# Weight preparation of a graph attention kernel: from GpSimd to VectorE by quarters, and the second adjacency product between the first masked ones

## What is computed

```python
# N = M = 4096, D = 128; adj holds 0 and 1, about 0.2% of them 1
e   = layernorm(x) @ a1 + (input2 @ a2).T          # N x M
e   = where(e > 0, e, 0.2 * e)
att = softmax(where(adj > 0, e, -9e15), axis=1)
att = 0.1 * att * sum(adj, axis=1, keepdims=True) + 0.9 * adj
x   = x + att @ input2
x   = x + layernorm(x) @ weight.T + bias
```

## Time and profile before

| | |
|---|---|
| time, median of 3 runs | 422.19 us (421.56 to 422.73) |
| the profiled execution's own time | 422.5 us |
| its span, first to last instruction | 420.7 us |
| mean granted TensorE clock | 0.972 |
| PE busy | 372.3 us (88%) |
| DVE busy | 359.4 us (85%) |
| ACT busy | 300.8 us (72%) |
| POOL busy | 127.2 us (30%) |

### The profile page before, as it was taken

The page is one execution under the profiler, slowest core; times in us unless marked ns, Lnnn a source line. Parts: engine busy times, 40 slices in busy tenths (PEclk is TensorE's granted clock), DMA queues, the critical chain, the costliest instruction groups (busy, mean ns, idle before and its releaser), DMA issues.

```text
span 420.7 us, 9474 instructions
## 1 busy us (share of the span) xinstructions
PE 372.3 (88%) x3237; PEld 322.4 (77%) x3237; DVE 359.4 (85%) x925; ACT 300.8 (72%) x534; POOL 127.2 (30%) x201
## 2 busy tenths in 40 slices
PE   0072759998999999999999999999999999999992
PEld 0061648876888888888888888888888888888881
DVE  3999999999999799897979797979898897979653
ACT  2465946999887969595959596987969595957000
POOL 2589931141414040505041221404040505010101
PEclk9996889998999999999999999999999999999996
DMA  6963173385583737473746556473737373600000
GB/s 229 423 241 104 78 291 137 123 302 182 176 301 119 287 142 247 154 274 109 275 154 240 196 209 227 151 285 107 281 148 240 143 276 107 221 15 0 15 2 27
DMA packets 17338, 76.11 MB, mean 181 GB/s; under 512 B 1936, under 2 KB 8608, under 8 KB 9120
## 3 DMA queue, kind: packets, MB, share of 16 engines
q1 hardware_dynamic: 17312, 75.78, 50.3%
HBM read 73.66 MB, written 2.11 MB: 180 GB/s over the span
## 4 chain that ended last, share of the span: by engine, by line
PE 75%; DVE 13%; ACT 4%; issue 3%; DMA 2%; POOL 1%; SPq 0%; POOLq 0%; ACTq 0%; DVEq 0%
PE acc_u L645 24%; PE acc_v L645 24%; PE acc_y L645 23%; DVE plus L789 3%; ACT steep L485 3%; DVE plus L925 2%; DVE weights_u L972 2%; PE small L639 2%; DMA plus<-in 2%; DVE plus L797 1%; PE small L625 1%; ACT adj_b L475 1%; PE turned L614 1%; DVE minus L800 1%; DVE minus L964 1%
## 5 line engine op out<-in xcount | busy, mean ns | idle before, releaser
L485 ACT ACTIVATE steep<-s_bc,steep_s 128x256 bf16<-128x256 f32 x376 | 156.0, 495 | 2.4 <-DVE plus L797 2.4
L645 PE MATMUL acc_y<-weights_y,adj_b 128*128 128x258 f16 x1024 | 123.7, 279 | 10.0 <-ACT adj_b L475 10.0
L645 PE MATMUL acc_u<-weights_u,plus 128*128 128x258 f16 x1024 | 122.5, 276 | 6.7 <-DVE plus L797 6.7
L475 ACT ACTIVATE adj_b<-stage 128x2048 bf16<-128x2048 f32 x64 | 121.3, 1900 | 1.5 <-DMA stage<-adj 1.4
L645 PEld LDWEIGHTS acc_y<-weights_y,adj_b 128*128 128x128 bf16 x1024 | 101.8, 100 | 26.9 <-ACT adj_b L475 10.6
L645 PE MATMUL acc_v<-weights_v,minus 128*128 128x258 f16 x1024 | 120.5, 273 | 0.0
L645 PEld LDWEIGHTS acc_u<-weights_u,plus 128*128 128x128 bf16 x1024 | 100.7, 99 | 22.9 <-DVE plus L797 7.3
L645 PEld LDWEIGHTS acc_v<-weights_v,minus 128*128 128x128 bf16 x1024 | 100.0, 98 | 14.6
L800 DVE TENSOR_TENSOR minus<-adj_b,plus 128x2048 bf16<-128x2048 bf16 x64 | 78.4, 1225 | 2.2
L498 ACT ACTIVATE num<-acc_u,ac 128x129 f32<-128x129 f32 x32 | 11.5, 361 | 81.8 <-PE acc_u L645 81.8
L385 POOL TENSOR_SCALAR post_var<-post_mv 128x2 f32<-128x2 f32 x16 | 3.4, 213 | 207.7 <-DVE post_mv L866 207.7
(11 more groups left out here) (82 smaller groups left out, 299.6 us busy)
## 6 DMA issues: line engine op xcount, KB each, us to landing
stage<-adj SPq DMA_DIRECT2D x64, 1024.0 KB, 4.8
plus<-in SPq DMA_DIRECT2D x4, 512.0 KB, 7.2
x_pre<-x SPq DMA_DIRECT2D x16, 128.0 KB, 2.5
x_res<-x SPq DMA_DIRECT2D x16, 128.0 KB, 2.4
out<-late SPq DMA_DIRECT2D x16, 128.0 KB, 5.0
s_rows<-s_bc SPq DMA_DIRECT2D x16, 1.0 KB
a_bc<-a SPq DMA_DIRECT2D x2, 64.0 KB, 3.8
wt_sb<-w_t SPq DMA_DIRECT2D x1, 64.0 KB, 13.3
```

The source lines that it names most:

```text
L475: nc.scalar.activation(adj_b[b][:, q * QJ:(q + 1) * QJ, :], stage[:, q, :], ACT.Copy)\
L485: ins = nc.scalar.activation(steep[:, h, k, :], s1_bc[b][:, :], ACT.Relu, bias=steep_s2[:, jt:jt + 1], scale=STEEP)
L645: ins = nc.tensor.matmul(acc[:, 0:2 * WC], left[:, jt, cols(t)], right[:, jt, :, :].rearrange("p a b -> p (a b)"), start=(jt == 0), stop=( ...
```

## The change

POOL keeps only small instructions: a new function factor_columns writes the column D of w_u and w_v. low_y, value_v and low_v of all quarters are DVE's. In DVE's program the preparation of a quarter stands between the comparison and the combination of chunk 0's masks. RJ0 goes, so chunk 0's quarters are split as all the others. The val buffers become four, two for u and two for v, of D columns. PE does spread(0, 0) first, and y of chunk 1 by quarters between chunk 0's masked products. The load of x_pre[1] moves behind the first adjacency quarter. The epilogues of chunk 0 move behind two mask quarters of chunk 1 on DVE and on ACT.

```diff
 @@ SP
-            for b in range(2):
-                sp.dma_start(x_pre[b][:, :, :], x[b]).then_inc(xpre_landed[b], 16)
+            sp.dma_start(x_pre[0][:, :, :], x[0]).then_inc(xpre_landed[0], 16)
             for q in range(1, QUARTERS):
                 sp.dma_start(in2_f[:, q * QJ:(q + 1) * QJ, :], in2[:, q]).then_inc(in2_landed[q], 16)
             load_adj(0, 0)
+            sp.dma_start(x_pre[1][:, :, :], x[1]).then_inc(xpre_landed[1], 16)
 @@ POOL
+            def factor_columns():
+                pool.wait_ge(bd_ready, 1)
+                nc.gpsimd.tensor_scalar(d_lifted[:, :], bd[:, 1, :], WSCALE, 1.0, ALU.mult, ALU.mult)\
+                    .then_inc(lifted, 1)
+                nc.gpsimd.tensor_scalar(b_lifted[:, :], bd[:, 0, :], WSCALE, 1.0, ALU.mult, ALU.mult)\
+                    .then_inc(lifted, 1)
+                pool.wait_ge(lifted, 2)
+                nc.gpsimd.tensor_copy(w_u[:, :, 0, D], b_lifted[:, :]).then_inc(lifted, 1)
+                nc.gpsimd.tensor_copy(w_v[:, :, 0, D], d_lifted[:, :]).then_inc(lifted, 1)
+                pool.wait_ge(lifted, 4)
+                nc.gpsimd.tensor_tensor(b_rest[:, :], b_lifted[:, :], w_u[:, :, 0, D],
+                                        ALU.subtract).then_inc(lifted, 1)
+                nc.gpsimd.tensor_tensor(w_v[:, :, 1, D], d_lifted[:, :], w_v[:, :, 0, D],
+                                        ALU.subtract).then_inc(factor_cols, 1)
+                pool.wait_ge(lifted, 5)
+                nc.gpsimd.tensor_scalar(w_u[:, :, 1, D], b_rest[:, :], LOSCALE, 1.0, ALU.mult, ALU.mult)\
+                    .then_inc(factor_cols, 1)
 
             row_sums(0, 0)
-            low_y(0)
-            low_y(1)
+            factor_columns()
             factors(0, 0, True)
-            pool.wait_ge(bd_ready, 1)
...
-            value_v(0)
-            value_v(1)
-            low_v(0)
             row_sums(1, 1)
             factors(1, 1, False)
-            for q in range(1, QUARTERS - 1):
-                value_v(q + 1)
-                low_v(q)
-            low_v(QUARTERS - 1)
 @@ ACT (after the four casts of w_y's high part), the order in the new kernel
+            copy_spread(0, 0)
             cast(0, 0, 0)
             act.wait_ge(bd_arg_ready, 2)
             nc.scalar.activation(bd[:, :, :], bd_arg[:, :, :], ACT.Exp).then_inc(bd_ready, 1)
             cast(0, 1, 0)
             act.wait_ge(s2_signs, 2)
+            act.wait_ge(s1_ready, 1)
             high_u(0)
+            high_v(0)
+            sign_tests(0, 0, 0)
+            cast(0, 2, 0)
             high_u(1)
+            high_v(1)
+            sign_tests(0, 1, 0)
+            cast(0, 3, 0)
+            copy_spread(1, 1)
             high_u(2)
+            high_v(2)
+            sign_tests(0, 2, 0)
+            cast(1, 0, 1)
+            cast(1, 1, 1)
             high_u(3)
+            high_v(3)
+            sign_tests(0, 3, 0)
             cast(1, 2, 1)
             cast(1, 3, 1)
+            exps(0, 0)
...
-                order = ["first", "second", 0, 1, 2, 3] if isinstance(c, int) and c == 0 else \
+                order = [0, 1, "first", "second", 2, 3] if isinstance(c, int) and c == 0 else \
 @@ PE
+            spread(0, 0)
             pe.wait_ge(smax_ready, 1)
...
             spread(1, 1)
             pe.wait_ge(g_ready, 1)
+            pe.wait_ge(factor_cols, 2)
             for q in range(QUARTERS):
...
                     if q == QUARTERS - 1:
                         ins.then_inc(tile_done, 1)
+                if q < 1:
+                    continue
+                if q == 1:
+                    pe.wait_ge(y_left, 2)
+                for p in [q - 1] if q < QUARTERS - 1 else [q - 1, q]:
+                    pe.wait_ge(cast_done, QUARTERS + p + 1)
+                    for t in range(TILES):
+                        ins = quarter(acc_y[t], adj_b[1], w_y, t, p)
+                        if p == QUARTERS - 1:
+                            ins.then_inc(y_done, 1)
+            spread(2, 0)
...
-                if ahead(c, 1):
+                if inner(c) and ahead(c, 1):
                     y_product(c + 1, 0, 1 - b)
 @@ DVE
+            def low_v(q):
+                qs = slice(q * QJ, (q + 1) * QJ)
+                dve.wait_ge(v_high, q + 1)
+                dve.wait_ge(v_val, q + 1)
+                nc.vector.tensor_tensor(w_v[:, qs, 1, 0:D], val_v[q % 2], w_v[:, qs, 0, 0:D],
+                                        ALU.subtract).then_inc(v_low, 1)
             nc.vector.tensor_reduce(s2_max[:, :], s2[:, :], AX.X, ALU.max).then_inc(smax_ready, 1)
+            low_y(0)
...
-            low_y(2)
+            low_y(1)
             dve.wait_ge(bd_ready, 1)
             value_u(0)
-            value_u(1)
-            pre_start(1, 1)
+            value_v(0)
+            low_y(2)
             dve.wait_ge(s2_signs, 2)
...
+            for q in range(QUARTERS):
+                compare(0, q, 0)
+                low_u(q)
+                low_v(q)
+                if q == 0:
+                    low_y(3)
+                if q < QUARTERS - 1:
+                    value_u(q + 1)
+                    value_v(q + 1)
+                if q == 0:
+                    pre_start(1, 1)
+                combine(0, q, 0)
+                if q == 1:
+                    for t in range(TILES):
+                        linear_part(0, t, 0)
...
-                order = ["compare", "first", "second", "combine", 1, 2, 3] if isinstance(c, int) and c == 0 else \
+                order = [0, 1, "first", "second", 2, 3] if isinstance(c, int) and c == 0 else \
```

More of the change, by code:

```diff
@@ L23 @@
 RJ = 6
-RJ0 = 4
 WC = D + 1
@@ L66, in gnn_ffn @@
         scratch = minus[1][:, :, :].rearrange("p a b -> p (a b)").bitcast(F32)
-        val = [scratch[:, b * QJ * WC:(b + 1) * QJ * WC].rearrange("p (t d) -> p t d", d=WC)
-               for b in range(3)]
+        val = [scratch[:, b * QJ * D:(b + 1) * QJ * D].rearrange("p (t d) -> p t d", d=D)
+               for b in range(4)]
+        val_u, val_v = val[0:2], val[2:4]
         late = sb("late", [P, 5, TILES * D], F32)
@@ L194, in gnn_ffn @@
         v_val = sem("v_val")
-        y_val = sem("y_val")
         lifted = sem("lifted")
+        factor_cols = sem("factor_cols")
         u_high = sem("u_high")
@@ L396, in post @@
                 last_add.then_inc(x1b_ready, 1)
[L398 to L421, removed]
@@ L476, in cast, with sign_tests @@
                     .then_inc(cast_done, 1)
-            def sign_tests(n, q, b, tests=RJ):
+            def sign_tests(n, q, b):
                 h = q % 2
@@ L482, in sign_tests @@
                     act.wait_ge(plus_ready, 4 * n + q - 1)
-                for k in range(tests):
-                    jt = (q + 1) * QJ - tests + k
+                for k in range(RJ):
+                    jt = (q + 1) * QJ - RJ + k
                     ins = nc.scalar.activation(steep[:, h, k, :], s1_bc[b][:, :], ACT.Relu,
@@ L520, in _, with high_u, high_v @@
                                      ACT.Copy, scale=WSCALE).then_inc(wy_high, 1)
+            def high_u(q):
+                act.wait_ge(u_val, q + 1)
+                nc.scalar.activation(w_u[:, q * QJ:(q + 1) * QJ, 0, 0:D], val_u[q % 2], ACT.Copy,
+                                     scale=1.0 / LOSCALE).then_inc(u_high, 1)
+            def high_v(q):
+                act.wait_ge(v_val, q + 1)
+                nc.scalar.activation(w_v[:, q * QJ:(q + 1) * QJ, 0, 0:D], val_v[q % 2], ACT.Copy).then_inc(v_high, 1)
+            copy_spread(0, 0)
             cast(0, 0, 0)
@@ L726, in slot @@
                     linear(c - 1)
-                if ahead(c, 1):
+                if inner(c) and ahead(c, 1):
                     y_product(c + 1, 1, 1 - b)
-                if not inner(c):
-                    spread(2, 0)
             run_slots(pe, slot)
@@ L783, in pre_start, with compare @@
                 ins.then_inc(pre_scaled, 1)
-            def compare(n, q, b, tests=RJ):
+            def compare(n, q, b):
                 dve.wait_ge(cast_done, 4 * n + q + 1)
-                for jt in range(q * QJ, (q + 1) * QJ - tests):
+                for jt in range(q * QJ, (q + 1) * QJ - RJ):
                     nc.vector.scalar_tensor_tensor(out=plus[b][:, jt, :], in0=s1_bc[b][:, :],
@@ L930, in _, with low_y, value_u @@
             ins.then_inc(s2_ready, 1)
+            def low_y(q):
+                qs = slice(q * QJ, (q + 1) * QJ)
+                dve.wait_ge(wy_high, q + 1)
+                nc.vector.scalar_tensor_tensor(out=w_y[:, qs, 1, 0:D], in0=in2_f[:, qs, :], scalar=WSCALE,
+                                               in1=w_y[:, qs, 0, 0:D], op0=ALU.mult,
+                                               op1=ALU.subtract).then_inc(wy_ready, 1)
+            def value_u(q):
+                qs = slice(q * QJ, (q + 1) * QJ)
+                if q >= 2:
+                    dve.wait_ge(u_low, q - 1)
+                nc.vector.scalar_tensor_tensor(
```

(38 more changed lines are left out.)

84 lines of the change are left out of this document (11 added, 73 removed).

## The result

The changed kernel took 411.32 us, the median of 4 runs (411.08 to 412.57), against 422.26 us before (421.56 to 422.73). The ratio is 0.9747, 95% interval 0.9727 to 0.9768. Another five runs in a later group gave 411.13 us and 0.9735. The forecast was 412.0 us, with 408.0 to 415.5 as its range. The profiled execution took 412.57 us with a span of 410.8 us; it is the slowest of its four, and the others have spans of 409.3 to 409.6.

What follows compares the result with a forecast made beforehand. VectorE's stream, held up by GpSimd's big instructions, was taken to bound the start. TensorE's earlier start (-8.1), removed idling and slowness (-3.8) and low clock (+1.7) cut the span from 420.7 to 410.5 us; forecast median 412.0, range 408.0 to 415.5.

Steps and rivals of the forecast that it cites:

- The place of the gain: Chunk 2's first masked product on TensorE starts at 91.8 us instead of 102.04; the 318.7 us behind it stay.
- idle stretch of 2.36 us: TensorE's idling at 96.27 us and the slow product after it, 2.4 + 1.4 = 3.8 us, go.
- ScalarE's last copy: ScalarE's copy of the turned rows comes at about 87 us, as TensorE gets there at 87.4, so no idling.
- GpSimd holds VectorE up: GpSimd's big preparation instructions stretch VectorE's at the start; without them VectorE loses 18.1 us, counting the dropped L964.
- The added instructions at 1.13 us each: VectorE gains ten instructions over 1024 elements (two low_y, four value_v, four low_v), 11.3 us in sum.
- Rival (c): VectorE's added instructions cost more: 415.7 us at 1.5 us each, 421.9 at 2.12; chance 0.05 in part.
- The end of the second epilogue: Chunk 0's epilogues end on VectorE at 67.1 us; TensorE starts chunk 1 there, 8.1 us earlier, after 6 us idle.
- The wait for ScalarE: VectorE reaches the combination of (1, 0) at about 55.5 us and waits 1.6 us for ScalarE's tests, done about 57.
- The low clock after the idle stretch: TensorE, after 6 us of idling ahead of chunk 1's masked products, loses some 1.7 us to a low clock.
- Rival (a): TensorE keeps its clock through y0 q3 and u1: 3.3 us more gain, 408.7 us; chance 0.20.
- Rival (d): GpSimd's 14 small instructions each let two VectorE ones pass, delaying row_sums(1, 1): 423 us; chance 0.05 shared with other losses.
- 3.2 us of comparisons less: Without the smaller RJ0, VectorE does 8 comparisons fewer at 0.40 us in chunk 0, 3.2 us less.

Runs made afterwards that it cites:

- run 6: Changed kernel with chunk 1's second adjacency product done as a whole behind chunk 0's masked products, not by quarters between them: 409.55 us.
- run 1: The changed kernel again, unaltered, in a later group of five executions: 411.13 us, ratio 0.9735.
- run 3: The kernel before, with only low_y of quarters 0 and 1 moved from GpSimd to VectorE: 418.23 us, ratio 0.9897.
- run 8: Changed kernel with chunk 0's two epilogues behind one mask quarter of chunk 1 instead of two, on VectorE and ScalarE: 412.66 us.
- run 2: Changed kernel with three added, unused GpSimd subtractions of 128x1024 beside VectorE's row sums: 416.51 us, ratio 0.9861.
- run 4: Changed kernel with value_v and low_v of all four quarters back on GpSimd (eight instructions): 416.51 us, ratio 0.9872.
- run 9: Changed kernel with chunk 0's epilogues one mask quarter earlier and ScalarE's copies of spread and turned rows right behind the numerators: 408.64 us.
- run 7: Changed kernel with spread(1, 1) on TensorE ahead of the last quarter of y of chunk 0: 411.05 us, ratio 0.9731.
- run 5: Changed kernel with RJ0 back to 4, so chunk 0's quarters have four sign tests and four comparisons: 413.07 us, ratio 0.9786.

## Why the prediction held

- **The place of the gain.** All of it lies ahead of chunk 2's first masked product, 92.24 us against the 91.8 worked out. Right. By terms, with the 22.7 us that run 6 needs from chunk 1's first masked product to chunk 2's (66.48 to 89.18) as the calm length: the earlier start gave 8.24 us (8.1 forecast), the idle stretch of 2.36 us and the slowness around it 4.13 (3.8 forecast), and the low clock took back 2.57 in the profiled execution and 1.66 in that of run 1 (1.7 forecast).
- **ScalarE's last copy.** Right, but barely: it was forecast at about 87 with TensorE there at 87.4, and it ends at 88.06 with TensorE there at 88.11. Runs 3 and 8 show what is lost without it, 3.97 and 3.89 us of idling. Which part of the change removed the stretch was not tested alone.
- **GpSimd holds VectorE up.** Right, and shown by run 2 (one cause added) and run 3 (one taken away). The row sums were forecast over by 14.7 us and are (14.71 for the maximum). One sign missed: GpSimd was to be busy under a third of its time before 66 us, and it is 20.30 us against 41.28, about half, because its small instructions are held too.
- **The added instructions at 1.13 us each.** Right: low_v is 1.22 busy, 1.13 to 1.15 from start to start. Rival (c) is out.
- **The end of the second epilogue.** 67.1 was worked out, 66.9 measured. Two terms in it were off. The wait for ScalarE was 0.77 us and not 1.6. A wait of 0.59 us at 28.6 wasn't in the sum: pre_start(1, 1) asks for GpSimd's factors(0, 0), a dependency in the code that I passed over. That they offset each other is no luck: ScalarE's tests of (1, 0) were worked out for about 57 us and VectorE went on behind them at 57.11, so whatever holds VectorE up ahead of them by less than that wait costs nothing. Past it, it does: in run 4 the wait for the factors grew to 5.42 us.
- **The low clock after the idle stretch.** 1.7 us were allowed, from one stretch of the trace before. The two groups behind it took 73.13 - 66.97 = 6.16 us against 3.58: 2.6 us in this profile, and 1.7 in that of run 1 (72.22 - 66.96 = 5.26). Rival (a) expected none; the profile of run 6 has that, with the stretch filled. Here the sum had luck: nothing in it could tell 1.7 from 2.6.
- **Rival (d), GpSimd shut out.** Its evidence didn't carry over. I wrote that a small instruction is held for one VectorE instruction, never two; pre_h took 2.08 us from 24.35. But that happened to one of the fourteen, row_sums(1, 1) was done at 31.65, and spread(1, 1) was wanted only after 37. The rival needed two for each.
- **The parts.** The forecast booked 3.2 us of comparisons less, against longer combinations, for the new split in chunk 0 (RJ0); undone, it costs 1.8 to 1.9 us. To the second adjacency product by quarters it gave nothing, and by run 6 it costs 1.6 to 1.8 us in the medians and 0.8 to 1.3 in the ratios, which isn't clear of the spread. The epilogues' new place and the order of preparation and masks were not undone alone, so how much of the gain is theirs stays open.

## What to carry to other kernels

Before a unit gets work because it is idle, look at what the busy unit's own instructions take beside it: here GpSimd's help cost more time than VectorE's own instructions for the same work, once the waits for GpSimd's queue are counted (run 4). When an engine's start is moved ahead, follow every wait that hangs on the end of the other engines' slots; a gain of 3 us at one point can end as a loss of 1.4 (run 8). An independent product may be worth most ahead of the longest idle stretch, where it kept TensorE's clock up in run 6, and not in the nearest gap.

## What the runs showed of the hardware

- A GpSimd subtraction of 128x1024 (2.06 us) holds one VectorE instruction for 1.97 us, and lets one of 0.28 us through at each change (run 2). The same rule of the Trainium skill (SBUF — State Buffer, on the shared port pair) shuts out the other engine for a whole instruction, and these rows agree.
- Small GpSimd instructions are held in turn: from 17.8 to 29 us of the changed kernel most of them take 0.8 to 1.3 us and pre_h takes 2.08, where the same pre_h takes 0.29 us at 56.6.
- The low clock doesn't follow from the length of the idle stretch ahead alone. After 6.07 and 5.95 us of idling, two groups lost 2.6 and 1.7 us; after 3.20 us (run 8) and 2.13 us (run 6) none; after 2.51 us (run 9) 1.6 (68.41 - 63.19 = 5.22 against 3.58). Equal stretches differ too: 5.40 us cost 2.3 in run 7 and 1.6 in run 5, and in run 3 a stretch of 3.20 us was followed by a slow group (3.37 us for 16 matmuls) and one of 3.14 was not (1.96).
